# A seventh buffer in a ring of gathered rows, with positions kept for four tiles and two buffers laid over each other

## What is computed

```python
wave = x @ wave_w.T + wave_b                       # 2*H columns per token, H = 8
# of sigmoid and tanh of it, averaged over heads: a frequency and a phase per token
pos = clip(base + phase + sidx * freq, 0, L - 1)   # 33 sample positions per token
lo, frac = floor(pos), pos - floor(pos)
sample = x[lo] * (1 - frac) + x[lo + 1] * frac     # two neighbouring rows
kern = silu(x @ kernel_w.T + kernel_b)             # a weight per head and sample
out = silu((kern * sample).sum(over the 33 samples) @ out_w.T)
x3 = layernorm(out + x)
```

## Time and profile before

| what | value |
|---|---|
| median of three runs | 1969.92 us (1968.27 to 1970.03) |
| the profiled execution, first to last instruction (no other time of it is recorded) | 2353.6 us |
| granted TensorE clock, mean | 0.854 of full speed |
| PE busy (x12145 matmuls) | 1720.4 us, 73% |
| DVE busy | 1254.1 us, 53% |
| POOL busy (x1069) | 1103.7 us, 47% |
| ACT busy | 988.0 us, 42% |
| chain that ended last | PE 39%, DVE 19%, a releaser that the trace does not name 18%, ACT 12%, POOL 1% |

### The profile page before, as it was taken

How to read it: one execution, slowest core, us unless ns; L and a number is a source line. 1 busy time by engine, 2 the same in 40 slices (tenths; PEclk the granted TensorE clock), 3 DMA queues, 4 the chain that set the end, 5 groups by cost and what they waited for, 6 DMA issues and landing times.

```text
span 2353.6 us, 31786 instructions
## 1 busy us (share of the span) xinstructions
PE 1720.4 (73%) x12145; PEld 1141.7 (49%) x12153; DVE 1254.1 (53%) x2158; ACT 988.0 (42%) x2363; POOL 1103.7 (47%) x1069
## 2 busy tenths in 40 slices
PE   5787876767777766666776766667787768879866
PEld 3354534445445534344555434454455346656645
DVE  6565645555556444555565545655565454343345
ACT  3365673234543551243353540335354533343333
POOL 0000016475556345664556255554665367766630
PEclk8799998778989877988898978789888879989876
DMA  3010023132223232232223232232233343223321
GB/s 133 10 24 14 19 48 96 58 102 83 79 75 103 63 74 79 79 96 73 88 79 90 56 95 70 83 90 72 86 89 85 69 148 99 88 81 90 88 47 36
DMA packets 93420, 178.72 MB, mean 76 GB/s; under 512 B 21452, under 2 KB 50264, under 8 KB 93016
## 3 DMA queue, kind: packets, MB, share of 16 engines
q0 software_dynamic: 50688, 138.48, 21.4%
q1 hardware_dynamic: 42584, 38.23, 5.8%
HBM read 151.46 MB, written 9.44 MB: 68 GB/s over the span
## 4 chain that ended last, share of the span: by engine, by line
PE 39%; DVE 19%; another core or an unknown queue 18%; ACT 12%; issue 9%; SPq 1%; POOL 1%; DMA 1%; DVEq 0%; POOLq 0%; ACTq 0%
PE c L1612 5%; DVE pool_c L1235 4%; PE pa L1508 3%; PE pb L1508 3%; PE ta L1542 2%; DVE ssq L1132 2%; PE ta L1516 2%; ACT pool_a L771 2%; ACT pool_a L836 2%; PE sc L1587 2%; DVE pool_a L1155 1%; DVE pool_a L1185 1%; PE tb L1389 1%; PE pb L1560 1%
## 5 line engine op out<-in xcount | busy, mean ns | idle before, releaser
L729 POOL DMA_INDIRECT pool_c<-rows_of_x,idx x1056 | 1100.9, 1043 | 1156.5 <-PE c L1612 380.0
L1612 PE MATMUL c<-ident,pool_c 128*128 128x128 f32 x2112 | 337.1, 303 | 61.6 <-DVE pool_c L1235 32.2
L1612 PEld LDWEIGHTS c<-ident,pool_c 128*128 128x128 f32 x2112 | 278.3, 158 | 143.0 <-issue 97.0
L1235 DVE TENSOR_TENSOR pool_c<-pool_c 128x768 f32<-128x768 f32 x352 | 331.3, 951 | 20.1 <-DMA pool_c<-rows_of_x,idx 19.7
L860 ACT ACTIVATE prob<-sc,nmax 128x128 f32<-128x128 f32 x512 | 179.3, 374 | 0.1
L1516 PE MATMUL ta<-ident,pool_a 128*128 128x128 f32 x512 | 90.9, 333 | 90.8 <-DVE pool_a L1155 80.4
L771 ACT COPY pool_a<-tb 128x512 f32<-128x512 f32 x188 | 112.5, 599 | 103.6 <-remote 58.3
L1155 DVE TENSOR_TENSOR pool_a<-ta,rinv 128x512 f32<-128x512 f32 x64 | 44.3, 692 | 199.9 <-remote 158.3
L1542 PE MATMUL ta<-vmix,pool_a 128*64 128x64 f32 x1024 | 80.9, 239 | 81.0 <-ACT pool_a L771 67.5
L1142 DVE TENSOR_REDUCE nmax<-sc 128x8 f32<-128x1024 f32 x64 | 77.5, 1211 | 103.9 <-remote 96.1
L1508 PE MATMUL pa<-wqkv,pool_a 128*128 128x512 f32 x192 | 118.8, 706 | 12.9 <-DVE pool_a L1185 7.4
(11 more groups left out here) (413 smaller groups left out, 3344.3 us busy)
## 6 DMA issues: line engine op xcount, KB each, us to landing
pool_c<-rows_of_x,idx POOLq DMA_INDIRECT x1056
vmix<-vring SPq DMA_DIRECT2D x128, 128.0 KB
rows_of_x<-x2tok SPq DMA_DIRECT2D x16, 256.0 KB
xtok<-in_x SPq DMA_DIRECT2D x4, 512.0 KB
x_of_all<-x2tok SPq DMA_DIRECT2D x8, 256.0 KB
out<-pool_c SPq DMA_DIRECT2D x8, 256.0 KB, 2.3
wqkv<-in_wqkv SPq DMA_DIRECT2D x1, 1536.0 KB
xtok<-x_of_all SPq DMA_DIRECT2D x3, 512.0 KB
```

The source lines that it names most:

```text
L729: pool.indirect_dma_start(gat[:, n % GB, s, :], None, tables[b % 2], bass.IndirectOffsetOnAxis(ap=idx[:, t, SC * c + s:SC * c + s + 1], ax ...
L1235: V.tensor_tensor(g4, g4, wv, ALU.mult).then_inc(SEM["c_prod"], 1)
L1612: ins = mm(out[:, c:c + P], x, ident[:], start=(i == 0 and k == 0), stop=(i == BCH - 1 and k == len(parts) - 1), is_transpose=True, skip_g ...
```

## The change

The ring gets seven slots. `pos` and `lo` shrink to four tiles and are written anew for the second half of a batch. `zc` becomes a view of `cT`, so ACT now waits for the x3 of the half before (`c_x3`) ahead of each copy of sums. The pool's total goes from 10144 numbers to 10136, and the ring begins 264 numbers lower.

```diff
-GB = 6
+GB = 7
...
-        pos = part("c", T, S)
-        lo = part("c", T, S)
-        tmp = pos
+        pos = part("c", TB, S)
+        lo = part("c", TB, S)
...
-        zc = part("c", TB, D)
         cT = part("c", BLK)
+        zc = cT.rearrange("p (t d) -> p t d", d=D)
...
                 elif what == "cT":
+                    wait(act, "c_x3", b, TB * a[0])
                     copy_out(("sum", a[0]), cT[:, :], b)
...
-                p4, l4, f4 = pos[:, ts], lo[:, ts], frac.rearrange("p (t s) c -> p t s c", t=T)[:, ts]
+                p4, l4, f4 = pos[:], lo[:], frac.rearrange("p (t s) c -> p t s c", t=T)[:, ts]
```

## The result

Nine timed runs of the changed kernel have a median of 1958.73 us (1946.42 to 1963.0), nine of the kernel before on the same chip 1968.27 (1962.6 to 1972.94). The ratio is 0.9939 with a 95% interval of 0.9917 to 0.9961: by it the change saves 12.0 us (7.7 to 16.3), where 9.7 were forecast. The two medians differ by 9.5 us, which lies in the same interval.

A forecast was written before the change was run, and what follows sets the result against it. The prediction took POOL's gathers to pace the tail and be close to late in the batches; terms of -2.2, -3.75 and -3.75 us summed to -9.7, from 1969.9 to a forecast of 1960 us, range 1945 to 1975.

The forecast's parts named there:

- one profile, two speeds: Whole span: 383.7 us belong to the profiled execution alone; without unnamed waits (414.2 us) POOL sets the tail's pace.
- The lead theory: Batches' late chunks and tail's ends: gathers set the pace; a slot is worth one chunk of gathers, 3.75 us, at each.
- Terms of zero: Four-tile positions and silu output in the sums' place, with ACT's second wait at seven copies: each taken as 0.
- Start of the tail, -2.2: Tail's seventh chunk: with a free slot its gather starts 2.24 us sooner; taken as -2.2 us, bounds 0 and -2.24.
- End of the tail, -3.75: Tail's last chunks: POOL enters its final run one chunk ahead, so the last landing comes 3.75 us sooner; bounds 2.4 and 7.6.
- In the batches, -3.75: Batch 1's product of chunk 33, otherwise 3.8 to 4.7 us late: -3.75 us, counted once; bounds 0 and -11.3.
- The sum: Whole kernel: -2.2 - 3.75 - 3.75 = -9.7 us, set against the median of the timed runs.
- The signs asked for: Changed profile: 21 gathers before POOL pauses, batch 1 pauses down some 20 us, tail-end waits 2 to 4 us shorter.
- No change: Whole kernel: POOL's pauses cost nothing where another engine is the bound; 1966 to 1974 us, chance 0.25.
- The slower rival: Batch heads and tail: gathers slow the engines beside them, 1.18 us a chunk; 1973.5 to 1981 us, chance 0.13.
- The larger gain: Tail and all three batches: two more chunks of lead in the tail, full -11.3 in the batches; 1945 us, chance 0.10.

The follow-up runs named there:

- seven without lead: Changed kernel with seven slots, but each gather still waits for the sums of the sixth chunk before it; ratio to the kernel before 0.9992.
- the shifted ring: Changed kernel with the ring moved up by 8 numbers (32 bytes), placed past a multiple of 256 bytes as before; ratio to the kernel before 0.9946.
- light gathers: Changed kernel's layout with six slots, a chunk's third gather left out except at a slot's first use in a batch; ratio to the kernel before 0.9677.

## Why the prediction was right, and where it was not

*The account behind it held in the main.* The step "one profile, two speeds" took the waits without a name as the profiled execution's own and inferred that in timed runs POOL paces the tail and is close to late in the batches. The second profile of the kernel before supports it: 1967.7 us, POOL with 33.6% of the tail's chain, and 11.3% of "issue", some nine tenths of it between gathers. PE has 40% of that chain, its pieces summed, so the pace is set by both, and not by POOL alone. The chain of that tail:

```profile
by line: POOL pool_c L729 33.6%; issue 11.3%; PE c L1612 8.6%; PE sc L1677 5.6%; DMA pool_c<-rows_of_x,idx 5.2%; PE pa L1684 2.7%; PE pb L1687 2.6%; PE ta L1682 2.4%; PE tb L1682 2.4%; PE tb L1684 2.3%; PE pa L1687 1.9%; PE pa L1682 1.6%; P
```

In the earlier trace rows POOL had 5.9% there. For the batches this chain says little, as it is followed back only to 1108 us; there the waits for rows, 14.1 to 16.0 us in each, show that gathers are late at times. The lead theory then survived the four runs that could have broken it (six slots in the new layout, seven without lead, the shifted ring, light gathers).

*Terms of zero: right.* Positions for four tiles and the silu in the sums' place, 0.9989 (0.9965 to 1.0014).

*Start of the tail, -2.2: right.* The seventh chunk waited 2.21 us with six slots (the row is below), and with seven it follows at 0.30. The wait of the ninth product, the first long one, went from 7.84 to 6.13 us, and from the tail's first product to this one it is 21.7 us (1545.29 to 1566.95) with six slots and 19.8 (1540.65 to 1560.41) with seven. POOL and DVE with six slots, then DVE with seven (timelines as in the earlier trace rows):

```profile
1547.51 0.94 POOL L729 DMA_INDIRECT pool_c<-rows_of_x,idx  x1 [2.21 <-PE c L1612]
...
1566.95 0.96 DVE L1235 TENSOR_TENSOR pool_c<-pool_c 128x768 f32<-128x768 f32 x1 [7.84 <-DMA pool_c<-rows_of_x,idx]
```

```profile
1560.41 1.02 DVE L1235 TENSOR_TENSOR pool_c<-pool_c 128x768 f32<-128x768 f32 x1 [6.13 <-DMA pool_c<-rows_of_x,idx]
```

*End of the tail, -3.75: the place wrong, the size not confirmed.* The waits of the last products did not shorten by 2 to 4 us: the last five wait 13.0 us with six slots and 13.6 with seven. POOL is late there in both, and what a slot gives has been given earlier, as pauses that vanish (2.21, 0.66, 2.17, 0.67 and 1.13 us between 1547 and 1742 us; with six of 0.3 us they make up the 8.7). Both tail terms together, 5.95 us, lie within the 3.5 to 11.8 of the timed runs and near the 5.4 us of real pauses; but the profiled tail became only 2.8 us shorter. With seven slots that stretch holds one gather more (247, not 246) and its gathers are longer on average (1.026 and 1.020 us), which takes back the rest. The 43.7 us that the prediction saw to draw on there came from the long execution.

*In the batches, -3.75: mechanism right, size open.* The step counted one late product, in batch 1 alone, and put the other batches at zero because they looked looser. In the timed runs the lead is worth 10.1 us (6.3 to 13.8) in the three batches. Waits for rows fall in each of them, by 3.9, 4.7 and 6.7 us, so counting one batch was wrong; the bound of -11.3 held. But the profiled batches became only 2.5 us shorter, so how much of those waits turns into time is not settled.

*The sum: partly luck.* With the end of the tail wrongly placed and one batch counted for three, it is partly luck that 9.7 came so near 12.0: the runs confirm the sign and the cause, not the division into terms. The price of a lead was also taken a little low: with gathers of 1.06 us on average a chunk takes 4.07 us, not 3.75.

*The signs asked for.* Twenty-one gathers went out before POOL paused at the head of batch 1, and that pause fell from 9.33 to 4.08 us:

```profile
756.31 1.02 POOL L729 DMA_INDIRECT pool_c<-rows_of_x,idx  x1 [9.33 <-PE c L1612]
```

```profile
754.75 1.03 POOL L728 DMA_INDIRECT pool_c<-rows_of_x,idx  x1 [4.08 <-PE c L1612]
```

POOL's pauses for sums in batch 1 fell by 9.4 us and not by 20: there were 31.1 us of them, not the 141.3 of the earlier trace rows. Its busy time there is 279.6 and 281.3 us, and the count stayed at 1056.

*The rivals.* No change fell to the intervals, and with it its argument from 19.7 us of waits, which are 141.4. The Trainium skill, "Perfetto Trace Analysis", section Identifying the Most-Contended Engine, says to optimise the engine with the highest occupancy first, but for TensorE to judge headroom by the busy share of its weight loads, or by its arithmetic rate, and not by that of its matmuls. The prediction used the matmuls' share. Over the whole changed kernel POOL (57%) comes first by neither: matmuls 81%, DVE 64%, weight loads 54%; yet leaving out gathers saved 3.2%. In the tail, with weight loads for TensorE, the trace agrees with it: POOL is busy 76%, weight loads 64%, DVE 45%, and POOL is taken up 98% once the 0.3 us between its gathers are counted. PE's matmuls are busy 87% there and have half of the chain. No run made PE or DVE faster, so what that would give is not shown. The slower rival priced gathers by the unnamed waits; no profile as long as the timed runs has them. The larger gain, 1945 us, lies beyond the 16.3 us of the interval; it rested in part on pauses in the tail that a normal execution does not have.

## What to carry to other kernels

Compare the span of a profile with the timed runs before reading waits in it; if it is much longer, the waits between engines are those of another balance, and a producer that is hidden in it may be the pace. In these runs another buffer in the ring paid only where the consumer waits for the producer and the producer pauses for the ring in the same stretch: pauses alone were worth nothing (460 us of them in the light kernel), and where the producer runs without a pause, as in this tail with seven slots, fewer gathers helped (64 us for nearly a third of them, the clock's part included) and an eighth buffer was not shown to. A wait that shrinks in a trace is not yet time saved: 41.5 us less waiting came with 12.0 us. Test such a buffer by keeping it and shortening the lead by one; that leaves layout and addresses as they are.

## What the runs showed of the hardware that was not expected

The same kernel was profiled at 2353.6 us and at 1967.7 us. POOL, DVE and ACT were busy nearly as long in both (1103.7 and 1112.3, 1254.1 and 1253.6, 988.0 and 982.1 us), PE 1720.4 and 1587.6, at a mean granted clock of 0.854 and 0.906, and 17.6% of the longer one stood in waits that no event explains. What made them is open. A gather of 128 rows takes POOL 0.95 us at the median but 1.06 on average, and at times 2.6 us. Gathers of batch 1 in the changed kernel (duration ns min/median/max, first and last start):

```profile
L728 POOL DMA_INDIRECT pool_c<-rows_of_x,idx x264: 942/949/2612, 754.8 to 1148.8; - x132
```

Over 1056 gathers the mean's excess over that median, 1057 - 949 ns, comes to 114 us, over nine times what the slot saved. What stretches them was not tried.
